# Another order of the same steps on four engines, and no bounds checks on fifteen loaded beginnings

## The chip, the cores and the metric

The kernel runs on one core of a Trainium2 chip. The metric is device time in microseconds (us) of one execution; the value given for a kernel is the median of several runs. A core has five engines with a queue of instructions each, TensorE (PE), VectorE (DVE), ScalarE (ACT), GpSimd (POOL) and SyncE (SP), and they meet only through semaphores.

## The reference, cut to what matters

Tokens `x` (2 x 1024 x 256) pass a cross attention with 16 heads over 77 keys, a feed-forward layer, a second cross attention with one head, and a layer in which each position goes through one of eight matrices, chosen by its position alone.

```python
x = x + _L0_xattn_ref(_layernorm(x), ctx_768, ...)   # 16 heads, 77 keys
x = x + _L0_ffn_ref(_layernorm(x), ...)              # only expert 0 has weight; then a layernorm
x = x + _L1_xattn_ref(_layernorm(x), ctx_768, ...)   # one head; layernorm of x and of the context
x = x + _L1_ffn_ref(_layernorm(x), ...)

# the router of the last layer
scores = jnp.einsum('sp,tp->st', pe, jnp.sign(tile_sigs))
idx = jnp.argmax(scores, axis=-1)
y_all = jnp.einsum('bsd,tod->bsto', x, W) + b
out = jnp.take_along_axis(y_all, idx4, axis=2)[:, :, 0]
```

## The kernel before, in words

The 2048 tokens are cut into eight groups `g` of 256, each with two halves of 128 rows. A group goes through a chain of short steps, and each engine works through **a list of such steps, written out by hand**: TensorE L522 to L552, VectorE L960 to L992, ScalarE L1136 to L1159, GpSimd L1319 to L1332. Each step is a small function that first waits for what it needs, works, and raises a semaphore. SyncE has its own loop of loads. Nothing but these lists and the waits sets the order.

The steps of a group, in the order of the data, with engine and line of VectorE's ones:

- Attention 1. `stats("A", g)` (VectorE, L597), `rs("A", g)` (GpSimd), `apply("A", g)` (one half of the group each on VectorE, L620, and ScalarE) normalise; `tA` (TensorE) transposes; `hi`/`lo("A", g)` (ScalarE/VectorE, L635) split the result in a high and a low part; `q`; `qh`/`ql(g)` (L641) split it; `sc(g, i, a)` scores; `smax` (L651), `ex` (ScalarE), `ssum` (L667), `en(g, i, a)` (GpSimd, L1259, two instructions each) softmax; `tE` transposes; `et`, `pv`, `o`, `wo`; `x1(g)` (L678) adds.
- Feed-forward. `stats`/`rs`/`apply("B", g)`, `tB`, `hi`/`lo("B", g)`; `w1(g, j)` for j = 0 to 3 (L412, twelve matmuls each, as products of high and low parts), `hh` (ScalarE) and `hl(g, j)` (VectorE, L683); `w2(g, i, h)` (L422); `y(g)` (L689), `stats`/`rs("Y", g)`, `x2(g)` (L695).
- Attention 2. `stats`/`rs`/`apply("C", g)`, `tC`, `xtc`, `cs`, `cm`, `cex`, `cp`, `cpt`, `co`, `x3_(g)` (VectorE).
- Last layer. `stats`/`rs`/`apply("D", g)`, `tD`, `xtd`. The tokens are then taken in the order of their matrix, as 15 pairs of (block of 128 tokens, matrix) for each half of the batch: `pc(b, r)` copies a pair's columns, `pr(b, r)` (L457) multiplies, `pa(b, r)` (L741) adds with a mask. Where a pair begins is an integer that the kernel works out itself: `r_pairs` (VectorE, L872 to L910), a chain of some 20 tiny dependent instructions. The last of them write `EV`; `load_starts` (L234) reads fifteen values into registers, on SyncE, and in `starts()` on VectorE (L737) and ScalarE (L1117), with a check of the bounds of each. The weights of the last layer (`load_weights`, SyncE) wait for this.
- Beside the groups: `mask`, `kf`, `kbl(b)` (L772), `vs`, `vb` prepare keys and values of attention 1; the steps that begin with `f_` do so for attention 2; those with `r_` route; `w_hi(n)` (ScalarE, L997) and `w_lo(n)` (GpSimd, L1194) split the weights of the feed-forward layer. The four parts of these weights are loaded in turn into two halves of one buffer, `RAW`: the third load waits for `w_lo(1)`, the fourth (`w2b`) for `w_lo(2)`, and `w_hi(4)` for the fourth.

TensorE writes to four PSUM banks `PB0` to `PB3`, and for `sc` and `tE` to one of two slots `S`. The last argument of a TensorE step is its bank. `hold` keeps the book: before a piece writes to a bank it waits for the step that empties the bank of its last piece (`w1(g, j)` for `hl(g, j)`, `wo(g)` for `x1(g)`, the `w2` of a group for `y(g)`):

```python
for signal, n in let_go.get(at, ()):
    w.wait_ge(s[signal], n)
place[piece] = at
let_go[at] = until
```

## Time and profile before

| | |
|---|---|
| median of 3 runs | 274.83 us (274.80 to 275.03) |
| span of the profiled execution | 271.97 us, 6214 instructions |
| PE busy | 249.2 us, 92% |
| DVE busy | 220.3 us, 81% |
| POOL busy | 189.7 us, 70% |
| ACT busy | 160.7 us, 59% |
| chain that ended last, by engine | PE 68%, DVE 15%, POOL 5%, ACT 5%, issue 4%, DMA 1% |
| mean granted clock of TensorE | 0.982 |

The span is the time from the first to the last instruction in the one execution that the profiler recorded; the runs are timed without the profiler, and some time around the span belongs to them. Busy shares are means over the whole span; the stages differ.

How to read the rows further down: an engine's timeline gives start, duration, engine, line, operation, tiles and shapes of each group of equal instructions, and in brackets the idle time before it and who ended it. The chain gives, in order of time, the pieces of work that the end of the program can be followed back to. In the table of stretches each engine has its busy time and, in brackets, its instructions. L266 are the products with high and low parts (`w1`, `w2`), L259 the plain ones (`q`, `wo`, `f_q`, `cs`), L339 the transposes of groups, L377 `sc`, L387 `tE`, L399 `pv`.

### The profile page before, as it was taken

The page shows a single profiled execution, that of the slowest core. Times are in us where ns is not written, and L with a number is a line of the kernel's source. Part 1 is how long each engine was busy: PE and PEld are TensorE (multiplying, and loading weights), DVE is VectorE, ACT ScalarE, POOL GpSimd, SP SyncE. Part 2 cuts the span into 40 slices and gives each one's busy share as a digit, 9 for nine tenths or more (in the row PEclk, how much of TensorE's full clock was granted, in tenths as well). Part 3 has the DMA queues.
Part 4 walks back from the last instruction along what each step waited for, and adds up shares of the span by engine and source line. Part 5 has one row for each costly group of instructions (what it writes and reads, how often), then busy time and mean ns, then how long its engine had stood idle before and what let it go on. Part 6 is the DMA issues. An engine that isn't in the chain of part 4 may idle for free.

```text
span 272.0 us, 6214 instructions
## 1 busy us (share of the span) xinstructions
PE 249.2 (92%) x2048; PEld 221.2 (81%) x2048; DVE 220.3 (81%) x573; ACT 160.7 (59%) x510; POOL 189.7 (70%) x361
## 2 busy tenths in 40 slices
...
DMA packets 11156, 17.61 MB, mean 65 GB/s; under 512 B 1377, under 2 KB 7509, under 8 KB 11125
## 3 DMA queue, kind: packets, MB, share of 16 engines
...
## 4 chain that ended last, share of the span: by engine, by line
PE 68%; DVE 15%; POOL 5%; ACT 5%; issue 4%; DMA 1%; SPq 0%; POOLq 0%; DVEq 0%; ACTq 0%
PE PB L266 29%; PE PB L259 12%; PE PB L464 9%; PE S L387 5%; PE PB L339 5%; PE PB L399 4%; PE S L377 4%; ACT E L1066 2%; DVE SX L659 2%; POOL E L1263 1%; DMA WKV<-in_w_k 1%; DVE SX L673 1%; POOL SM L1220 1%; DVE HL L686 1%; DVE XTL L638 1%
## 5 line engine op out<-in xcount | busy, mean ns | idle before, releaser
L1263 POOL TENSOR_TENSOR E<-E,SX 128x308 f32<-128x308 f32 x64 | 43.8, 712 | 10.7 <-DVE SX L676 10.4
L1066 ACT ACTIVATE E<-S,SX 128x77 f32<-128x77 f32 x128 | 39.4, 336 | 10.6 <-DVE SX L659 10.6
L266 PE MATMUL PB<-XTH,W1H 128*128 128x256 f32 x128 | 37.7, 295 | 1.5 <-DVE XTL L638 1.4
L266 PE MATMUL PB<-W2H,HH 128*128 128x256 f32 x128 | 37.6, 294 | 0.0
L266 PE MATMUL PB<-XTL,W1H 128*128 128x256 f32 x128 | 36.2, 283 | 0.0
L266 PE MATMUL PB<-XTH,W1L 128*128 128x256 f32 x128 | 36.2, 282 | 0.0
L266 PE MATMUL PB<-W2H,HL 128*128 128x256 f32 x128 | 35.5, 278 | 0.0
L266 PE MATMUL PB<-W2L,HH 128*128 128x256 f32 x128 | 35.5, 278 | 0.0
L1220 POOL TENSOR_TENSOR SM<-SM,nhalf 128x2 f32<-128x2 f32 x40 | 28.3, 707 | 3.1
L1089 ACT ACTIVATE HH<-PB 128x512 fp32r<-128x512 f32 x32 | 19.0, 598 | 18.0 <-PE PB L266 18.0
L1076 ACT ACTIVATE EW<-S 124x640 f32<-124x640 f32 x32 | 21.9, 711 | 10.9 <-PE S L387 10.1
L1066 ACT ACTIVATION_READ_ACCUMULATOR E<-S,SX 128x1 f32 x128 | 27.9, 218 | 0.0
L266 PEld LDWEIGHTS PB<-XTH,W1H 128*128 128x128 f32 x128 | 24.4, 191 | 2.3 <-DVE XTL L638 1.6
L615 DVE BATCH_NORM_STATS2 SM<-X 128x6 f32<-128x256 f32 x64 | 23.8, 413 | 2.1 <-DMA X<-in_x 1.3
L659 DVE TENSOR_REDUCE SX<-S 128x8 f32<-128x616 f32 x32 | 24.4, 783 | 1.0 <-PE S L377 1.0
L266 PEld LDWEIGHTS PB<-W2H,HH 128*128 128x128 f32 x128 | 24.1, 188 | 1.3 <-issue 1.2
L266 PEld LDWEIGHTS PB<-XTL,W1H 128*128 128x128 f32 x128 | 24.5, 191 | 0.1
L266 PEld LDWEIGHTS PB<-XTH,W1L 128*128 128x128 f32 x128 | 24.5, 191 | 0.0
L1033 ACT ACTIVATE XN<-X,SM 128x256 f32<-128x256 f32 (+1 forms) x32 | 18.6, 601 | 9.7 <-POOL SM L1226 9.7
L266 PEld LDWEIGHTS PB<-W2L,HH 128*128 128x128 f32 x128 | 24.1, 189 | 0.1
L1217 POOL TENSOR_TENSOR SM<-SM,eps 128x2 f32<-128x2 f32 x32 | 6.6, 205 | 25.3 <-DVE SM L618 25.1
L266 PEld LDWEIGHTS PB<-W2H,HL 128*128 128x128 f32 x128 | 24.0, 188 | 0.0
...
## 6 DMA issues: line engine op xcount, KB each, us to landing
RAW<-in_w SPq DMA_DIRECT2D x4, 512.0 KB, 6.3
...
X<-in_w1r SPq DMA_DIRECT2D x1, 512.0 KB, 6.6
...
```

The lines of the kernel that those rows point to most:

```text
L259: t = e.matmul(dst, a, b, start=j == 0, stop=j == len(pairs) - 1)
L266: t = e.matmul(dst, a, b, start=first and j == 0, stop=last and j == n - 1)
L339: t = e.transpose(P[:, c * 256 + i * 128:c * 256 + (i + 1) * 128], xn[:, i, c * 128:(c + 1) * 128], ident[:, :])
L464: t = e.matmul(P[:, v * 256:(v + 1) * 256], XP[:, TURN[b, r] % 2, v, c * 128:(c + 1) * 128], weights_of(n)[:, c * 256:(c + 1) * 256], star ...
L615: step(e.bn_stats(smi(K, g, i, 0, 6), src[:, i, :]))
L659: e.tensor_reduce(top, sv, AX, ALU.max, negate=True).then_inc(s["mx"], 1)
L1033: e.activation(dst_of(K, g)[:, 1, 0:n], src_of(K, g)[:, 1, 0:n], ACT.Identity, bias=smi(K, g, 1, 10, 11), scale=smi(K, g, 1, 9, 10)).then_ ...
L1066: t = e.activation(Ei[:, h * NK:(h + 1) * NK], P[:, at:at + NK], ACT.Exp, bias=SX[:, i, 0, k:k + 1], accum_out=SX[:, i, 1, k:k + 1])
L1076: e.activation(ET[:, g % 2, a, :, ts], P[0:CW, 0:640].rearrange("p (c t) -> p c t", c=5), ACT.Copy).then_inc(s["et"], 1)
L1089: e.activation(HH[:, 2 * j:2 * j + 2, :], two(bank("w1", g, j)[:, :]), ACT.Relu).then_inc(s["hh"], 1)
L1220: e.tensor_tensor(sm(K, g, 9), sm(K, g, 8), nhalf[:, :], ALU.pow).then_inc(s["rs" + K], 1)
L1263: t = e.tensor_tensor(Eh, Eh, SX[:, i, 2, 8 * a + h:8 * a + h + 4].unsqueeze(2).to_broadcast([128, 4, NK]), ALU.mult)
```

## The change

Two things. The reading of the fifteen beginnings no longer checks their bounds. And the lists of steps on TensorE, VectorE, ScalarE and GpSimd hold the same steps as before in another order (246, 274, 218 and 142 steps), many pieces of TensorE in another bank. SyncE's list stays. No step is added, dropped or changed.

The diff, cut to the places that the text speaks of (in this order: the reading, TensorE old and new, VectorE old and new, ScalarE old and new, GpSimd old and new):

```diff
         def load_starts(e, row, most, at):
 
             values = nc.values_load_multi_w_load_instructions(EV[0:1, row, 0:NP], engines=[e.engine],
-                                                              min_val=0, max_val=most)[1]
+                                                              min_val=0, max_val=most, skip_runtime_bounds_check_because=
+                                                              "a count of 7 comparisons times a positive constant")[1]
...
-            sc(2, 1, 0, 1); sc(2, 1, 1, 0); pv(1, 1); r_perm(1); w1(0, 0, 3); wo(1, 0); w1(0, 1, 2); w1(0, 2, 1)
-            w1(0, 3, 3); f_m(0); tE(2, 0, 0, 0); tA(3, 2); w2(0, 0, 0, 1); tE(2, 0, 1, 1); tB(1, 0); w2(0, 0, 1)
-            w2(0, 1, 0); q(3, 2); w2(0, 1, 1); w1(1, 0, 3); sc(3, 0, 0, 1); sc(3, 0, 1, 0); w1(1, 1, 0); w1(1, 2, 2)
-            tE(2, 1, 0, 0); f_q(3); w1(1, 3, 1); tE(2, 1, 1, 1); f_c(); sc(3, 1, 0, 0); sc(3, 1, 1, 1); pv(2, 0, 0)
-            pv(2, 1); w2(1, 0, 0, 2); w2(1, 0, 1); tA(4, 3); w2(1, 1, 0); w2(1, 1, 1); wo(2, 1); tE(3, 0, 0, 0)
-            f_o(3); tE(3, 0, 1, 1); q(4, 0); tE(3, 1, 0, 1); tA(5, 3); tE(3, 1, 1, 0); pv(3, 0, 1); pv(3, 1)
-            sc(4, 0, 0, 1); sc(4, 0, 1, 0); tB(2, 2); wo(3, 1); q(5, 0); w1(2, 0, 3); w1(2, 1, 1); w1(2, 2, 2)
...
-            cs(5, 3); w1(7, 0, 2); tD(2, 1); w1(7, 1, 3); w1(7, 2, 0); w1(7, 3, 1); cp(5, 3); w2(7, 0, 0, 2); co(5)
-            tD(3, 0); w2(7, 0, 1); w2(7, 1, 0); w2(7, 1, 1); tC(6, 0); tD(4, 3); pr(0, 1, 1); cs(6, 2); pr(0, 2, 3)
...
+            pv(1, 1); sc(2, 0, 1, 1); sc(2, 1, 0, 0); r_perm(2); tB(0, 1); wo(1, 3); tE(2, 0, 0, 1); f_q(1)
+            w1(0, 0, 3); w1(0, 1, 2); w1(0, 2, 0); sc(2, 1, 1, 1); sc(3, 0, 0, 0); f_c(); w1(0, 3, 2); tB(1, 3)
+            w2(0, 0, 0, 1); tE(2, 0, 1, 1); w2(0, 0, 1); w1(1, 0, 0); tE(2, 1, 0, 0); w2(0, 1, 0); w2(0, 1, 1)
+            w1(1, 1, 3); w1(1, 2, 2); tE(2, 1, 1, 1); sc(3, 0, 1, 0); pv(2, 0, 0); pv(2, 1); sc(3, 1, 0, 0)
+            sc(3, 1, 1, 1); w1(1, 3, 0); f_o(3); wo(2, 2); tA(4, 1); w2(1, 0, 0, 0); tE(3, 0, 0, 0); w2(1, 0, 1)
+            q(4, 1); tE(3, 0, 1, 0); w2(1, 1, 0); w2(1, 1, 1); tE(3, 1, 0, 1); tB(2, 3); tE(3, 1, 1, 0); tA(5, 2)
+            sc(4, 0, 0, 1); sc(4, 0, 1, 0); pv(3, 0, 0); pv(3, 1); tC(0, 1); w1(2, 0, 3); w1(2, 1, 1)
...
+            w2(6, 1, 0); w2(6, 1, 1); co(4); tB(7, 1); tC(5, 2); pr(0, 0, 3); w1(7, 0, 0); tD(2, 1); w1(7, 1, 3)
+            cs(5, 2); w1(7, 2, 0); w1(7, 3, 1); w2(7, 0, 0, 3); cp(5, 2); w2(7, 0, 1); tD(3, 1); co(5); w2(7, 1, 0)
+            w2(7, 1, 1); tC(6, 1); cs(6, 3); pr(0, 1, 0); tD(4, 1); pr(0, 2, 2); cp(6, 3); tC(7, 0); co(6); cs(7, 2)
...
-            ssum(1, 1, 0); stats("B", 0); r_position(); smax(2, 0, 0); ssum(1, 1, 1); apply("B", 0); smax(2, 0, 1)
-            f_kv(0); f_kv(1); vb(1); lo("B", 0); ssum(2, 0, 0); smax(2, 1, 0); smax(2, 1, 1); kbl(1); r_index()
-            ssum(2, 0, 1); apply("A", 3); hl(0, 0); hl(0, 1); x1(1); ssum(2, 1, 0); stats("B", 1); hl(0, 2); f_m()
-            hl(0, 3); apply("B", 1); lo("A", 3); r_pairs(); lo("B", 1); ssum(2, 1, 1); ql(3); y(0); stats("A", 4)
-            smax(3, 0, 0); smax(3, 0, 1); hl(1, 0); apply("A", 4); stats("Y", 0); f_q(); hl(1, 1); x2(0)
-            ssum(3, 0, 0); ssum(3, 0, 1); hl(1, 2); hl(1, 3); f_c(); stats("C", 0); smax(3, 1, 0); smax(3, 1, 1)
-            lo("A", 4); stats("A", 5); stats("A", 6); y(1); apply("A", 5); x1(2); ssum(3, 1, 0); ssum(3, 1, 1)
-            stats("B", 2); f_o(); stats("Y", 1); stats("A", 7); ql(4); apply("B", 2); x2(1); lo("A", 5); smax(4, 0, 0)
...
-            smax(5, 0, 0); ssum(4, 0, 1); lo("B", 3); ssum(4, 1, 0); cm(0); ssum(4, 1, 1); apply("C", 1); starts()
...
-            apply("C", 5); x3_(4); lo("B", 7); apply("D", 2); y(6); stats("D", 4); cm(5); hl(7, 0); stats("Y", 6)
-            hl(7, 1); apply("D", 3); x2(6); hl(7, 2); hl(7, 3); stats("C", 6); x3_(5); stats("D", 5); apply("C", 6)
...
+            smax(1, 1, 1); ssum(1, 1, 0); lo("A", 3); r_expert(); smax(2, 0, 0); f_kv(0); ssum(1, 1, 1); x1(0)
+            f_kv(1); stats("B", 0); ssum(2, 0, 0); r_position(); apply("B", 0); ql(3); smax(2, 0, 1); lo("B", 0)
+            smax(2, 1, 0); x1(1); r_index(); f_m(); ssum(2, 0, 1); stats("B", 1); ssum(2, 1, 0); f_q(); hl(0, 0)
+            hl(0, 1); smax(2, 1, 1); f_c(); apply("B", 1); smax(3, 0, 0); hl(0, 2); hl(0, 3); lo("B", 1)
+            ssum(2, 1, 1); stats("A", 4); r_pairs(); hl(1, 0); ssum(3, 0, 0); hl(1, 1); smax(3, 0, 1); y(0)
+            hl(1, 2); smax(3, 1, 0); ssum(3, 0, 1); stats("Y", 0); apply("A", 4); hl(1, 3); x2(0); f_o()
+            ssum(3, 1, 0); stats("A", 5); lo("A", 4); stats("C", 0); x1(2); smax(3, 1, 1); stats("B", 2)
+            apply("C", 0); ssum(3, 1, 1); apply("B", 2); kbl(1); apply("A", 5); ql(4); y(1); smax(4, 0, 0)
+            stats("A", 6); lo("B", 2); stats("Y", 1); lo("A", 5); smax(4, 0, 1); stats("A", 7); hl(2, 0); hl(2, 1)
...
+            x2(5); hl(6, 0); hl(6, 1); starts(); hl(6, 2); stats("C", 5); hl(6, 3); apply("C", 5); stats("D", 2)
...
+            lo("B", 7); pa(0, 0); apply("D", 3); stats("D", 4); hl(7, 0); cm(5); stats("Y", 6); hl(7, 1); hl(7, 2)
+            hl(7, 3); x2(6); stats("C", 6); x3_(5); stats("D", 5); apply("C", 6); apply("D", 4); y(7); stats("Y", 7)
...
-            ex(1, 1, 1); et(1, 0, 0); et(1, 0, 1); et(1, 1, 0); f_ct(); apply("B", 0); w_hi(4); ex(2, 0, 0)
-            et(1, 1, 1); hi("B", 0); apply("A", 3); o(1); ex(2, 0, 1); ex(2, 1, 0); hh(0, 0); hh(0, 1); ex(2, 1, 1)
...
-            starts(); hi("A", 4); o(2); ex(3, 1, 0); ex(3, 1, 1); apply("C", 0); et(3, 0, 0); apply("A", 5)
...
+            f_ct(); hi("A", 3); et(1, 0, 0); w_hi(2); ex(1, 1, 1); w_hi(3); ex(2, 0, 0); et(1, 0, 1); et(1, 1, 0)
+            qh(3); et(1, 1, 1); o(1); apply("B", 0); w_hi(4); hi("B", 0); ex(2, 0, 1); et(2, 0, 0); ex(2, 1, 0)
...
+            apply("B", 4); cpt(1); ex(5, 1, 1); et(5, 0, 1); hi("A", 7); xtc(2); hi("B", 4); et(5, 1, 0); starts()
...
-            setup(); rs("A", 0); rs("A", 1); bo(0); rs("A", 2); r_iota(); w_lo(1); bo(1); en(0, 0, 0); en(0, 0, 1)
-            en(0, 1, 0); f_rs(); en(0, 1, 1); w_lo(2); f_gb(); en(1, 0, 0); en(1, 0, 1); en(1, 1, 0); rs("A", 3)
-            rs("B", 0); en(1, 1, 1); w_lo(3); w_lo(4); en(2, 0, 0); bo(2); en(2, 0, 1); en(2, 1, 0); rs("B", 1); gx(4)
...
+            setup(); rs("A", 0); rs("A", 1); r_iota(); rs("A", 2); en(0, 0, 0); en(0, 0, 1); bo(0); en(0, 1, 0)
+            rs("A", 3); f_rs(); en(0, 1, 1); w_lo(1); f_gb(); en(1, 0, 0); bo(1); en(1, 0, 1); en(1, 1, 0); w_lo(2)
+            en(1, 1, 1); rs("B", 0); en(2, 0, 0); w_lo(3); w_lo(4); en(2, 0, 1); rs("B", 1); gx(4); en(2, 1, 0)
```

## Rows read from the trace of the kernel before

**Rows 1.** Stretches: us, busy PE, PEld, DVE, ACT, POOL; PE clock, DMA share, GB/s.
```profile
30.20:72.20 42.00, 39.00 (x379) 33.22 (x379) 39.64 (x103) 28.47 (x99) 35.57 (x56) 1.00 0.11 33
100.00:217.60 117.60, 117.60 (x1036) 107.90 (x1025) 94.78 (x238) 73.61 (x242) 86.05 (x167) 1.00 0.18 53
```
**Rows 2.** The chain that ended last, 72 to 104 us: start, us, what.
```profile
72.23 1.69 PE PB L266 x12
73.92 1.09 PE S L377 x12
...
78.61 0.79 PE PB L259 x8
...
87.86 0.44 PE PB L339 x4
88.30 2.73 PE PB L266 x24
...
95.03 0.55 PE S L387 x5
95.58 1.43 PE PB L266 x12
...
98.53 1.93 PE PB L399 x32
```
**Rows 3.** VectorE's timeline, 51 to 76 us.
```profile
51.38 0.69 DVE L638 TENSOR_TENSOR XTL<-PB,XTH 128x512 fp32r<-128x512 f32 x1 [0.58 <-ACT XTH L1041]
...
54.30 1.65 DVE L775 TENSOR_TENSOR KBL<-XTE,mask 128x308 fp32r<-128x308 f32 x2
...
64.12 0.17 DVE L874 SCALAR_TENSOR_TENSOR WD<-WD 128x16 f32<-128x16 f32 x1
...
71.50 0.68 DVE L638 TENSOR_TENSOR XTL<-PB,XTH 128x512 fp32r<-128x512 f32 x1
...
75.31 1.47 DVE L659 TENSOR_REDUCE SX<-S 128x8 f32<-128x616 f32 x2
```
**Rows 4.** VectorE's timeline, 88 to 99 us.
```profile
88.96 0.69 DVE L638 TENSOR_TENSOR XTL<-PB,XTH 128x512 fp32r<-128x512 f32 x1 [1.16 <-ACT XTH L1041]
...
91.44 0.66 DVE L693 TENSOR_TENSOR XN<-PB,XN 128x512 f32<-128x512 f32 x1
...
96.87 0.72 DVE L615 BATCH_NORM_STATS2 SM<-X 128x6 f32<-128x256 f32 x2
...
97.92 0.88 DVE L646 SCALAR_TENSOR_TENSOR XTL<-PB,cols,XTH 128x256 fp32r<-128x256 f32 x2
```
**Rows 5.** VectorE's timeline, 220 to 233 us.
```profile
220.40 0.69 DVE L686 SCALAR_TENSOR_TENSOR HL<-PB,HH 128x512 fp32r<-128x512 f32 x1 [0.50 <-ACT HH L1089]
...
221.72 1.83 DVE L699 SCALAR_TENSOR_TENSOR XN<-XN,SM,bc 128x256 f32<-128x256 f32 x2
...
225.22 1.27 DVE L686 SCALAR_TENSOR_TENSOR HL<-PB,HH 128x512 fp32r<-128x512 f32 x2
...
231.02 0.69 DVE L693 TENSOR_TENSOR XN<-PB,XN 128x512 f32<-128x512 f32 x1 [0.44 <-PE PB L266]
...
232.81 0.91 DVE L699 SCALAR_TENSOR_TENSOR XN<-XN,SM,bc 128x256 f32<-128x256 f32 x2
```
**Rows 6.** TensorE's timeline at 226 us.
```profile
226.04 0.63 PE L339 MATMUL PB<-ident,XN 128*128 128x128 f32 x4 [1.23 <-DVE HL L686]
```
**Rows 7.** Line 236: durations min/median/max in ns, first and last start.
```profile
L236 DVEq FUSED_REGOPS  x15: 183/183/206, 120.9 to 124.8; - x15
```
**Rows 8.** GpSimd's timeline at 32 us.
```profile
32.29 3.18 POOL L1202 TENSOR_TENSOR W1L<-RAW,W1H 128x256 fp32r<-128x256 f32 x4
```
**Rows 9.** The page: costliest groups (busy, mean ns, idle before) and DMA issues.
```profile
L1263 POOL TENSOR_TENSOR E<-E,SX 128x308 f32<-128x308 f32 x64 | 43.8, 712 | 10.7 <-DVE SX L676 10.4
...
RAW<-in_w SPq DMA_DIRECT2D x4, 512.0 KB, 6.3
```
**Rows 10.** ScalarE's timeline at 47 us.
```profile
46.78 1.04 ACT L1006 ACTIVATE W2H<-RAW 128x1024 fp32r<-128x1024 f32 x1
```

152 lines of the change are left out of this document (76 added, 76 removed).

## The prediction

> **What bounds the kernel now.** I began with the busy time of each engine by stage. From 100 to 217.6 us TensorE is busy all of the time; between 30.2 and 72.2 it is VectorE that is nearly full (39.64 of 42.00) while TensorE loses 3 us [rows 1]. In the second stretch only fewer TensorE pieces could help; in the first VectorE's order decides when TensorE gets its operands. Next I followed the chain of waits. It leaves VectorE for the last time before the long stretch at 71.50, with `lo("B", 1)` [rows 3], and from `w1(1, 0)` at 72.23 on it is TensorE's alone until 217.6 [rows 2, 1]. **Where `w1(1, 0)` starts sets all that follows**, as long as nobody makes TensorE wait again. Near the end VectorE is back: TensorE stands 1.23 us before the transpose at 226.04, waiting for a `hl` [rows 6] that is queued behind `x2(6)` [rows 5]. After that a chain of dependent steps of the last group, in the same order in both kernels, sets the end.
>
> **The change part by part.** The sum is made against the profiled execution: its span is 271.97 us, and the median of the runs, 274.83, lies 2.86 above it. I add the 2.86 back at the end.
>
> *Head, VectorE.* All of `r_pairs` stood ahead of `lo("B", 1)`, from 64.12 to 71.50: 7.38 us. It now comes behind. So does `kbl(1)`, 1.57 us from its start at 54.30 to the next step [rows 3]. Ahead of it come `ql(3)` (0.79, as `ql(4)` from 97.92 to 98.71 [rows 4]), one `smax` more (0.74, half of the pair at 75.31 [rows 3]), and the small `f_q` and `f_c` (0.6 together, an estimate from steps of their size): 2.1. VectorE alone would reach the end of `lo("B", 1)` at 72.17 - 8.95 + 2.1 = 65.3, which is 6.9 earlier.
>
> *Head, TensorE.* It does not get there so soon. `lo("B", 0)` ended at 52.07 [rows 3]. Ahead of it there are now `apply("A", 3)` (0.3, half of `y(1)`, which has twice its elements and took 91.44 to 92.01 [rows 4]), `lo("A", 3)` (0.6), `ql(3)` (0.8) and a part of a `ssum` (0.1): 1.8. Then `smax(2, 1, 0)` (0.7) and `x1(1)` (0.6) must be done before `w1(0, 0)` may start, since it is now written to bank 3, which `x1(1)` empties. That gives 55.2, or 54.2 if the idle 0.58 before `lo("B", 0)` [rows 3] and another such wait vanish; I take 55.1. From there to `w1(1, 0)` TensorE has four `w1` of 1.43, two `sc` (1.09 together), `f_c` (0.4, half of the matmuls of `f_q`), `tB(1)` (0.44), two `w2` (2.73) and a `tE` (0.55) [rows 2]: 10.9 us, and 0.3 for starting behind others. So `w1(1, 0)` starts at 66.3 against 72.23: **5.9 earlier**. But more work is left behind it: two `w2` (2.73) went behind, `f_q` (0.79), one `sc` (0.54) and `f_c` came ahead [rows 2], 0.9 to 1.0 more is left. Net **-5.0**. Bounds: VectorE's 6.9 less the same 0.9 is -6.0; if `w1(0, 0)` comes a microsecond later than I say, -4.0.
>
> *Second hold.* TensorE now comes 5 us sooner to `sc(4, 0, 0)`, which needs `ql(4)`. Today `ql(4)` ends at 98.80 [rows 4] and `sc(4, 0, 0)` starts at 100.46, behind the `pv` that began at 98.53 [rows 2]: 1.7 us of slack, less than what TensorE gains. Three `stats` (0.92 to 1.05 each, as 96.87 to 97.92) and `y(1)` (0.57) leave the way to `ql(4)`, 3.5 in all; two `apply` (0.6) enter [rows 4]. So it ends at 95.9 if VectorE gets no faster otherwise, and TensorE would be there at 100.46 - 5.0 - 1.93 (`pv(3)` now behind) + 0.44 (a `tB` now ahead) = 94.0, late by 1.9. Of VectorE's time up to there 1.16, the idle before the step at 88.96 [rows 4], hangs on steps that TensorE feeds and should shrink: 0.7. I take **+1.0**, nearer to 0.7 because that wait is one which TensorE's own lateness makes; ends 0.4 and 1.9.
>
> *End.* `hl(7, 2)` and `hl(7, 3)` now stand ahead of `x2(6)` (221.72 to 225.22 [rows 5]), so the wait of 1.23 us [rows 6] goes. What is late next is `y(7)`. It started at 231.02 with only 0.44 of waiting for TensorE [rows 5], so VectorE was ready at 230.58, and an earlier TensorE can bring it 0.44 and no more, while VectorE's steps from 221.72 on stay the same. And they now start later: `hl(7, 3)` cannot be done before about 1.4 us after the last `w1` of the group, 223.7 on the old clock, where `x2(6)` plus the two `hl` of 0.6 started at 221.72. So `y(7)` comes at 223.7 + (230.58 - 221.72 - 1.2) = 231.4 on the old clock: 0.3 later, unless `x2(6)` loses its slow form. Its first two instructions took 1.83 where those of `x2(7)`, the same shape, took 0.91 [rows 5]; at that price some 1.7 go, TensorE is the last again, and -1.2 is left. I take **-0.3**, nearer to the row as it is; ends +0.3 and -1.2.
>
> The Trainium skill, "SBUF — State Buffer", section "Who interferes with whom", has VectorE and GpSimd share a pair of ports under an exclusive lock, so that the loser stands still. The 1.83 against 0.91 agrees with it, and by this rule `x2(6)` would be as slow wherever GpSimd is at work on it, which would make the end +0.3.
>
> *Bounds checks.* VectorE's sequencer has 15 checks, 183 ns each, between 120.9 and 125.0 [rows 7]; SyncE and ScalarE have as many. All lie where TensorE never stands still [rows 1]: that is the cover, and I take **0**. Without it VectorE's stop, 15 x 0.27 = 4.1 us, would cost what exceeds its lead over TensorE. The reads of the registers on VectorE and ScalarE also move, into the same covered stretch. *Other banks.* A bank has one owner at a time; where a new bank makes a wait that I can place, it is counted (`w1(0, 0)`). For the rest I take 0, between 0 and 0.5.
>
> **Sum**: -5.0 + 1.0 - 0.3 = -4.3; a span of 267.7 and a median of 270.5 us, 1.6% faster.
>
> **Rivals.**
> - *Part is given back.* The second hold costs its 1.9, the end +0.3, and one more step in VectorE's new stretch doubles as `x2(6)` did, 0.8: -5.0 + 1.9 + 0.3 + 0.8 = -2.0, 272.8. For it: VectorE is the full engine up to 72 us [rows 1], so what lengthens there counts. Against: such steps were lengthened before too.
> - *More comes.* TensorE takes VectorE's 6.9 at the head, the second hold is gone, and the end gives its 1.2: -6.0 - 1.2 = -7.2; 267.6. For it: the waits of VectorE that TensorE makes [rows 3, 4]. Against: it needs `w1(0, 0)` at 54.
> - *Slower.* `w_lo(2)` on GpSimd ran from 32.29 to 35.47 [rows 8]. Now `rs("A", 3)` (2), `f_gb` (2) and three `en` of two 0.7 us steps each [rows 9] go ahead of it, besides others ahead of `w_lo(1)`: it ends at about 44. The load into the buffer that it frees lands 6.3 us later [rows 9], `w_hi(4)` waits for that, takes 1.0 [rows 10], and stands on ScalarE ahead of `hi("B", 0)` (0.6), without which there is no `lo("B", 0)`. So `lo("B", 0)` starts 7.9 us after the end of `w_lo(2)` at the earliest: 52, where I count with 53.3. It decides from 45.4 on; at 49.7 the gain of 4.3 is gone, and at 51.7, with GpSimd's steps ahead of it at nearly twice their time, the kernel is 2 slower: 276.8.
> - *No change.* TensorE's waits form anew behind VectorE: what left the way to `lo("B", 1)` is due soon after, and VectorE's work up to `y(2)` is the same. It needs the second hold to be 5 instead of 1. 274.8.
>
> **Chances.** The forecast 0.60, part given back 0.20, more 0.07, slower 0.08, no change 0.05. A measurement of this kernel can tell about 0.2%, 0.55 us, from no change. Faster 0.87, same 0.05, slower 0.08. The range goes from 267.3 (just beyond the second rival: head -6.0, end -1.2, 0.3 of small waits) to 273.5 (head -4.0, hold +1.9, end +0.3, 0.5 for banks: -1.3); outside are the slower case, no change and a tail of the one given back.
>
> **What the profile of the changed kernel would show.** Head: `lo("B", 1)` ends at 65 to 66, `w1(1, 0)` starts near 66.3, `r_pairs` behind them. Hold: TensorE idle for about 1 us before `sc(4, 0, 0)`, at 94 to 96. End: no idle time before the transpose of `tD(3)`; `y(7)` near 226.7 instead of 231.0, held by VectorE's own steps; the last piece on TensorE near 261. No checks on any sequencer. TensorE full from about 97 to 212. It would be wrong if `w1(1, 0)` started after 69, or if TensorE showed new idle time between 100 and 200 us; a `w_hi(4)` that ends after 54 would be the slower case.

## The result, and the profile of the changed kernel

The changed kernel is slower. It took 284.57 us (median of 4 runs, 282.94 to 284.84) beside 274.89 us (4 runs, 274.80 to 275.03) for the kernel before: ratio 1.033 (95% interval 1.031 to 1.036). Run again it took 282.58 us (4 runs, 281.15 to 289.45), ratio 1.028 (1.024 to 1.032). Of the runs of one kernel some are over 1.5% slower than the fastest, at a lower clock (here the one of 289.45 us, in experiment 4 one of 296.65); the ratios leave them out. The forecast was 270.5 us, range 267.3 to 273.5. It had the wrong sign.

The first lines of its page:

```profile
span 283.0 us, 6131 instructions
## 1 busy us (share of the span) xinstructions
PE 253.0 (89%) x2048; PEld 224.2 (79%) x2048; DVE 228.1 (81%) x573; ACT 160.7 (57%) x510; POOL 193.0 (68%) x361
```

The counts of instructions on each engine are those of before; only the register and check instructions are fewer. Yet VectorE is busy 7.8 us longer (228.1 against 220.3) and TensorE 3.8 (253.0 against 249.2). The span has grown by 11.0 us. TensorE works or stands idle, so 3.8 of them are slower work and 7.2 are new idle time. The mean granted clock was 0.970 over 283.0 us against 0.982 over 272.0, which makes some 3.6 us of the 3.8 (an estimate). The table of stretches says where (columns as in [rows 1]; the second fence is the kernel before in the two stretches that its rows don't show):

```profile
5.70:30.20 24.50, 19.26 (x125) 16.84 (x126) 20.49 (x57) 14.25 (x51) 11.60 (x25) 0.93 0.66 195
30.20:72.20 42.00, 36.58 (x329) 30.15 (x328) 36.80 (x84) 27.70 (x93) 31.24 (x49) 0.88 0.10 32
72.20:100.00 27.80, 27.30 (x240) 24.95 (x240) 26.70 (x66) 15.25 (x51) 23.37 (x37) 1.00 0.28 92
100.00:217.60 117.60, 114.74 (x1025) 104.13 (x1024) 98.17 (x242) 74.29 (x244) 89.40 (x172) 1.00 0.15 45
217.60:283.00 65.40, 55.06 (x337) 48.05 (x335) 44.65 (x116) 27.23 (x69) 35.25 (x70) 0.97 0.11 42
```
```profile
5.70:30.20 24.50, 20.48 (x123) 17.13 (x123) 22.54 (x61) 16.82 (x54) 14.35 (x30) 0.86 0.70 217
217.60:272.00 54.40, 44.30 (x262) 38.41 (x260) 36.24 (x92) 23.44 (x62) 29.81 (x53) 0.97 0.10 39
```

TensorE's idle time, stretch less PE: 5.2 us before 30.2 (4.0 in the kernel before), 5.4 from 30.2 to 72.2 (3.0), 0.5 to 100 (0), 2.9 from 100 to 217.6 (0 [rows 1]), 10.3 behind (10.1). So the head costs 3.6 us, the stretch from 72 on, which was full before, 3.4, and the end 0.2.

This is one execution. A second one of the same kernel had its clock at the upper level from 30 to 72 us throughout. Its span was 279.8 us, 7.8 above before: 1.8 more idle time up to 72.2 us, 3.5 from there to 217.6, 0.3 at the end, and 2.2 of slower work. Where a time depends on the clock of the head, this second execution is the better measure, and it is given beside the first.

The head in TensorE's timeline (the kernels without checks have TensorE's lines one higher, L267 for L266 and so on, and the changed kernel VectorE's by one or two):

```profile
39.25 0.47 PE L476 MATMUL PB<-ident,CKN 77*96 77x77 f32 x4 [1.37 <-POOL CKN L1242]
41.40 1.11 PE L340 MATMUL PB<-ident,XN 128*128 128x128 f32 x4 [1.68 <-DVE XN L634]
42.31 3.62 PE L260 MATMUL PB<-Wo,RT 128*128 128x256 f32 x8
...
59.11 0.36 PE L326 MATMUL PB<-WD 128*128 128x16 bf16 x8 [0.71 <-DVE WD L858]
60.76 0.80 PE L340 MATMUL PB<-ident,XN 128*128 128x128 f32 x4 [1.28 <-DVE XTL L648]
```

They are `f_turn`, `tA(3)`, `wo(0)`, `r_perm` and `tB(0)`. `w1(0, 0)` follows at 65.99 (52.75 before, 55.1 forecast), `lo("B", 1)` ends at 75.90 (72.17; forecast 65 to 66) and `w1(1, 0)` starts at 77.33 (72.23; forecast 66.3). In the second execution the three are at 62.50, 72.40 and 73.87. It has these rows for `lo("B", 0)` and `w1(0, 0)`:

```profile
60.26 0.68 DVE L640 TENSOR_TENSOR XTL<-PB,XTH 128x512 fp32r<-128x512 f32 x1
62.50 0.36 PE L267 MATMUL PB<-XTH,W1H 128*128 128x256 f32 x1
```

The third row of the first fence shows TensorE's clock: eight matmuls took 3.62 us, against 1.89 in the second execution. Between 38 and 41.4 us TensorE had worked 0.47 us of 3.4. The clock granted fell to its lower level, 1.2 GHz, for a part of the time: the mean was 0.88 of the full 2.4 GHz in this stretch and 0.70 in the next.

```profile
38.00:41.40 3.40, 0.47 (x4) 0.31 (x5) 3.40 (x5) 2.85 (x17) 3.32 (x6) 0.88 0.51 154
41.40:51.60 10.20, 10.20 (x86) 9.02 (x86) 7.71 (x20) 5.17 (x15) 5.85 (x9) 0.70 0.01 2
```

In the stretch that was full before, TensorE now waits four times, for GpSimd's softmax step once and for VectorE's low parts twice:

```profile
104.27 0.63 PE L340 MATMUL PB<-ident,XN 128*128 128x128 f32 x4 [0.29 <-issue]
105.58 0.76 PE L388 MATMUL S<-ident,E 128*124 128x128 f32 x5 [0.68 <-POOL E L1266]
...
123.64 1.12 PE L260 MATMUL PB<-M,XN 128*128 128x77 f32 x8 [0.74 <-DVE XTL L648]
...
135.12 0.39 PE L267 MATMUL PB<-XTH,W1H 128*128 128x256 f32 x1 [0.93 <-DVE XTL L640]
```

Where 4.1 of VectorE's 7.8 us went, at two places, and below them the answering rows of before. From its start to the next one `apply("A", 3)` took 2.46 us against 0.29, and `r_position` 5.60 against 3.69. `f_norm` took 1.0 more, and the rest is spread over later steps.

```profile
38.81 2.54 DVE L634 TENSOR_SCALAR XN<-X,SM 128x256 f32<-128x256 f32 x1
...
55.79 1.68 DVE L854 TENSOR_TENSOR WD<-WD 128x1024 bf16<-128x1024 f32 x1
57.39 0.75 DVE L855 TENSOR_TENSOR WD<-WD 128x64 f32<-128x64 f32 x1
58.18 0.74 DVE L857 TENSOR_SCALAR WD<-WD 128x64 bf16<-128x64 f32 x1
58.84 0.21 DVE L858 TENSOR_TENSOR WD<-WD 128x64 bf16<-128x64 f32 x1
```
```profile
43.54 1.22 DVE L852 TENSOR_TENSOR WD<-WD 128x1024 bf16<-128x1024 f32 x1
44.69 0.22 DVE L853 TENSOR_TENSOR WD<-WD 128x64 f32<-128x64 f32 x1
44.94 0.26 DVE L855 TENSOR_SCALAR WD<-WD 128x64 bf16<-128x64 f32 x1
...
58.08 0.38 DVE L632 TENSOR_SCALAR XN<-X,SM 128x256 f32<-128x256 f32 x1
```

Beside `apply("A", 3)` GpSimd runs `f_gb`, two instructions of `en(1, 0, 0)` and the first of `bo(1)`. The last four rows of the first fence belong to `r_position`, and beside them GpSimd runs the four pieces of `w_lo(3)`, from 56.35 for 4.13 us. Steps of 64 elements that take 0.22 us alone take 0.75, about as long as one of GpSimd's. The engines do not meet through semaphores alone.

### The profile page after: what moved, and what is told of

It reads as the page before. It is cut to its first block, busy times and chain, and to the rows that moved or that the text cites. A ratio compares the mean times of both kernels' runs of the same rounds, so it can differ in the third digit from the quotient of the medians.

```text
span 283.0 us, 6131 instructions
## 1 busy us (share of the span) xinstructions
PE 253.0 (89%) x2048; PEld 224.2 (79%) x2048; DVE 228.1 (81%) x573; ACT 160.7 (57%) x510; POOL 193.0 (68%) x361
## 3 DMA queue, kind: packets, MB, share of 16 engines
HBM read 14.07 MB, written 3.15 MB: 61 GB/s over the span
## 4 chain that ended last, share of the span: by engine, by line
PE 44%; DVE 29%; issue 8%; DMA 7%; POOL 7%; SPq 1%; ACT 1%; POOLq 0%; DVEq 0%
PE PB L267 16%; PE PB L260 9%; PE PB L465 7%; DVE SM L617 4%; PE PB L340 4%; DMA CKN<-in_ctx 4%; DVE SX L661 3%; PE PB L400 3%; PE S L388 3%; DVE XN L634 2%; PE S L378 2%; POOL E L1266 2%; DVE X L707 2%; POOL SM L1223 2%; DMA X<-in_x,SI 2%
## 5 line engine op out<-in xcount | busy, mean ns | idle before, releaser
L1266 POOL TENSOR_TENSOR E<-E,SX 128x308 f32<-128x308 f32 x64 | 45.6, 735 | 16.1 <-DVE SX L678 15.9
L267 PE MATMUL PB<-XTH,W1H 128*128 128x256 f32 x128 | 38.2, 298 | 0.9 <-DVE XTL L640 0.9
L267 PE MATMUL PB<-W2H,HH 128*128 128x256 f32 x128 | 37.6, 294 | 0.0
L267 PE MATMUL PB<-XTL,W1H 128*128 128x256 f32 x128 | 36.1, 282 | 0.0
L267 PE MATMUL PB<-XTH,W1L 128*128 128x256 f32 x128 | 36.1, 282 | 0.0
L267 PE MATMUL PB<-W2L,HH 128*128 128x256 f32 x128 | 35.6, 278 | 0.0
L267 PE MATMUL PB<-W2H,HL 128*128 128x256 f32 x128 | 35.6, 278 | 0.0
L1078 ACT ACTIVATE EW<-S 124x640 f32<-124x640 f32 x32 | 22.7, 712 | 17.2 <-PE S L388 17.2
L1220 POOL TENSOR_TENSOR SM<-SM,eps 128x2 f32<-128x2 f32 x32 | 7.6, 238 | 29.8 <-DVE SM L620 29.6
L388 PE MATMUL S<-ident,E 128*124 128x128 f32 x160 | 23.4, 278 | 4.3 <-POOL E L1266 2.5
L267 PEld LDWEIGHTS PB<-XTH,W1H 128*128 128x128 f32 x128 | 24.4, 191 | 2.2 <-DVE XTL L640 1.2
L340 PE MATMUL PB<-ident,XN 128*128 128x128 f32 x128 | 20.5, 288 | 5.0 <-DVE XN L634 3.0
L267 PEld LDWEIGHTS PB<-W2H,HH 128*128 128x128 f32 x128 | 24.1, 189 | 0.7 <-issue 0.6
L267 PEld LDWEIGHTS PB<-XTL,W1H 128*128 128x128 f32 x128 | 24.5, 191 | 0.1
L267 PEld LDWEIGHTS PB<-XTH,W1L 128*128 128x128 f32 x128 | 24.4, 191 | 0.0
```

The source lines that it names most:

```text
L267: t = e.matmul(dst, a, b, start=first and j == 0, stop=last and j == n - 1)
L340: t = e.transpose(P[:, c * 256 + i * 128:c * 256 + (i + 1) * 128], xn[:, i, c * 128:(c + 1) * 128], ident[:, :])
L388: t = e.transpose(P[0:CW, c * 128:(c + 1) * 128], E[:, i, a, c * CW:(c + 1) * CW], ident[:, :])
L1078: e.activation(ET[:, g % 2, a, :, ts], P[0:CW, 0:640].rearrange("p (c t) -> p c t", c=5), ACT.Copy).then_inc(s["et"], 1)
L1266: t = e.tensor_tensor(Eh, Eh, SX[:, i, 2, 8 * a + h:8 * a + h + 4].unsqueeze(2).to_broadcast([128, 4, NK]), ALU.mult)
```

## The experiments

Runs of the changed kernel spread by some 2 us within a series, those of before by 1.0 to 2.2. So variants of the changed kernel are compared by places in the trace, and by medians only within one series. The profiled executions differ in the clock of the head, so such a place is compared with both executions of the changed kernel.

**1. The bounds checks alone.** The order of before, with the change to `load_starts`:

```diff
-                                                              min_val=0, max_val=most)[1]
+                                                              min_val=0, max_val=most, skip_runtime_bounds_check_because=
+                                                              "a count of 7 comparisons times a positive constant")[1]
```

> The order of before, only the bounds checks gone. If the checks are covered, as forecast, 274.6 to 275.0 and no sequencer shows them. If they or the earlier load of the last layer's weights matter in themselves, the time moves by more than 0.5 us either way, and the order alone did less or more than the change shows.

275.16 us (10 runs, 274.48 to 275.93), ratio 1.001 (0.999 to 1.003). The checks cost nothing that can be told from zero within 0.3%; all that follows is order.

**2. `r_pairs` alone.** In the order of before:

```diff
-... lo("A", 3); r_pairs(); lo("B", 1) ...
+... lo("A", 3); lo("B", 1) ...
-... f_q(); hl(1, 1); x2(0)
+... f_q(); hl(1, 1); r_pairs(); x2(0)
-... smax(2, 1, 1); kbl(1); r_index()
+... smax(2, 1, 1); r_index()
-... stats("A", 7); ql(4); ...
+... stats("A", 7); kbl(1); ql(4); ...
```

> The order of before, only with r_pairs behind lo("B", 1) and the first two hl of group 1, and kbl(1) just ahead of ql(4). If my step for the head holds (what leaves the way to lo("B", 1) is gained), w1(1, 0) starts at 66 to 68 and the kernel takes 270 to 272. If r_pairs only moves its 7.4 us to the next step that is due (x2, smax, hl of group 1), TensorE waits there instead and the time is 274 to 277.

279.69 us (4 runs), ratio 1.018 (1.015 to 1.021). VectorE and TensorE in this kernel:

```profile
66.18 0.69 DVE L638 TENSOR_TENSOR XTL<-PB,XTH 128x512 fp32r<-128x512 f32 x1 [1.69 <-ACT XTH L1041]
70.64 0.88 DVE L646 SCALAR_TENSOR_TENSOR XTL<-PB,cols,XTH 128x256 fp32r<-128x256 f32 x2 [2.83 <-ACT XTH L1049]
```
```profile
87.70 0.55 PE L266 MATMUL PB<-W2H,HH 128*128 128x256 f32 x1 [4.20 <-DVE HL L686]
```

`lo("B", 1)` came 5.3 us sooner, much as I had reckoned for VectorE alone. `w1(1, 0)` came only 1.3 sooner, at 70.94: TensorE was busy with the pieces ahead of it, without a gap. And behind it TensorE stood 4.2 us: its piece `w2(1, 0, 0)` goes to bank 2, which `hl(1, 2)` empties, and this now waited behind `r_pairs`. The wait did not go; it moved and grew. It also cost the clock. The 24 matmuls behind it ran at the lower level and took 5.2 us, where 24 such took 2.73 in the kernel before [rows 2]:

```profile
87.70:92.90 5.20, 5.20 (x24) 5.20 (x25) 3.77 (x9) 0.00 (x0) 3.65 (x8) 0.50 0.00 0
```

So the price is above both of the ranges expected.

**3. `r_pairs` far behind.** Without checks, at about 140 us, with `starts()` on VectorE and ScalarE and `bs(0)` on GpSimd behind it:

```diff
-... lo("A", 3); r_pairs(); lo("B", 1) ...
+... lo("A", 3); lo("B", 1) ...
-... ssum(4, 1, 1); apply("C", 1); starts()
+... ssum(4, 1, 1); apply("C", 1)
-... ssum(5, 1, 1); apply("C", 2) ...
+... ssum(5, 1, 1); r_pairs(); starts(); apply("C", 2) ...
-... en(4, 0, 0); bs(0); en(4, 0, 1) ...
+... en(4, 0, 0); en(4, 0, 1) ...
```

> The order of before without bounds checks, with r_pairs far behind, at about 140 us, where VectorE has idle time, and with the readings of the registers and the first indirect load of the bias behind it. New theory: TensorE's own work up to w1(1, 0) does not shrink, so the most that can be gained is its idle 1.42 us before w1(1, 0), and the work of 7.4 us is free only here: 272.8 to 273.6. Old theory (VectorE's time off the way to lo("B", 1) is gained): 269 to 271. Rival (the 7.4 us have to be paid on VectorE wherever they stand): 274.5 or more.

282.49 us (4 runs), ratio 1.026 (1.024 to 1.029). Both theories were wrong; the rival (274.5 or more) has the direction, without a price. From 73 to 142 us TensorE ran 0.9 us ahead of the kernel before. Then one wait took 6.6 us:

```profile
148.78 1.09 PE L340 MATMUL PB<-ident,XN 128*128 128x128 f32 x4 [6.58 <-DVE XN L694]
```
```profile
147.62 0.41 DVE L633 TENSOR_SCALAR XN<-X,SM 128x256 f32<-128x256 f32 x1 [1.69 <-issue]
```

It is `tC(2)`, which needs `apply("C", 2)` and a bank that `y(3)` empties; both stood behind `r_pairs` and `starts()`. The edit is no clean case of `r_pairs`: `starts()` now reads its registers right behind it, and 1.69 us of VectorE's lump of 7.74 are that reading (the second row), with 6.0 for `r_pairs`. Behind the wait the granted clock was 0.50 for 5 us more, an estimate of 2.6 us. VectorE has idle time in this stretch (it is busy 94.78 of 117.60 us [rows 1]), but in waits of at most 3.6 us, mostly for TensorE (the trace of experiment 1). Its lead is never 7 us.

**4. The same in the changed kernel** (ScalarE's `starts()` behind `o(5)`, GpSimd's `bs(0)` to `bs(5)` in a row behind `rs("Y", 3)`).

```diff
-... stats("A", 4); r_pairs(); hl(1, 0) ...
+... stats("A", 4); hl(1, 0) ...
-... ssum(5, 1, 1); smax(6, 0, 0) ...
+... ssum(5, 1, 1); r_pairs(); smax(6, 0, 0) ...
```

> The changed kernel, with r_pairs at about 155 us in place of 78 to 86, and what waits for it behind. If TensorE's idle 2.9 us between 100 and 136 come from VectorE being full from 50 to 145 us, of which these 7.6 us are a part, they go, and the kernel takes 281 to 282. If they come from the order around them, 284 to 285.

288.77 us (4 runs), ratio 1.049 (1.045 to 1.053), above both of the ranges expected. From 100 to 139 us TensorE gained 1.3 us on the changed kernel's own course: the wait of 0.93 at 135 went, those at 104, 106 and 124 stayed at 0.23, 0.68 and 0.63. So up to half of that stretch's loss goes with `r_pairs`; then `w1(4, 0)` waited 4.12 us.

**5. TensorE's idle time at 38 to 41 us.** In the changed kernel, one `wo` ahead of the waiting pieces, then both:

```diff
-... f_turn(1); tA(3, 0); wo(0, 2); ...
+... wo(0, 2); f_turn(1); tA(3, 0); ...
-... r_perm(2); tB(0, 1); wo(1, 3); ...
+... wo(1, 3); r_perm(2); tB(0, 1); ...
```

> The changed kernel, only with wo(0) of TensorE ahead of f_turn and tA(3), which it stands idle for between 38 and 41.4 us before the granted clock falls to 1.2 GHz for some 5 us. If that idle time and the clock are what makes the head late, the clock stays at 2.4 GHz in 41 to 52 us, w1(0, 0) comes 3 to 4 us sooner and the kernel takes 280 to 282. If GpSimd and VectorE hold the head up, w1(0, 0) moves by under 1 us and the time stays at 284 to 285.

> The changed kernel with wo(0) ahead of f_turn and tA(3), and wo(1) ahead of r_perm and tB(0), on TensorE. Both wo have their data when TensorE stands idle. If the head is late because TensorE's list has waiting pieces ahead of ready ones, the idle 1.8 us at r_perm and tB(0) go as well: 280.5 to 281.5. If VectorE, which does its routing steps ahead of apply("B", 0), sets the pace, it is as with wo(0) alone, 282.5 to 283.5.

282.90 us (1.031, 1.027 to 1.034) and 282.62 us (1.027, 1.024 to 1.030). The clock stayed at its upper level in 41.4 to 51.6 us with the first edit, and `sc(2, 0, 0)` came 4.7 us sooner than in the first execution of the changed kernel. But `w1(0, 0)` gained only 2.2, half of it there at 29 us already, and 3.6 with both edits. Even this is the clock: the unedited kernel, run again, had no drop of the clock in this stretch, and there `w1(0, 0)` starts at 62.50 and `lo("B", 0)` ends at 60.94, against 62.42 and 60.97 with both edits. Both times `lo("B", 0)` ends behind VectorE's own steps, which had no gap from `r_position` to `apply("B", 0)`. So the order of these pieces ahead of `tB(0)` is not what sets the head. The unedited kernel, run again, had a span of 279.8 us instead of 283.0, but stood idle for 6.1 us here, against 5.4:

```profile
30.20:72.20 42.00, 35.93 (x360) 30.40 (x361) 40.36 (x91) 30.44 (x103) 34.27 (x54) 1.00 0.13 39
```

The clock explains some 3 us of the first profile. It does not explain the sign.

**6. `bo(1)` out of the way of `apply("A", 3)`**, in the changed kernel (on GpSimd ahead of `w_lo(1)`, 8 us sooner).

```diff
-... en(0, 1, 1); w_lo(1); f_gb(); en(1, 0, 0); bo(1) ...
+... en(0, 1, 1); bo(1); w_lo(1); f_gb(); en(1, 0, 0) ...
```

> The changed kernel with bo(1) of GpSimd, two additions, ahead of w_lo(1), about 8 us sooner, so that it no longer stands beside VectorE's apply("A", 3), which took 2.46 us where it took 0.29 in the kernel before. If GpSimd's bo(1) holds VectorE up, the step takes under 1.2 us, tA(3) comes over 1 us sooner and the time falls by 1 to 3 us, the more the clock stays up. If another GpSimd step takes bo(1)'s place beside it, the step stays above 2 us and the time at 283 to 285.

283.64 us (282.03 to 284.67), ratio 1.032 (1.028 to 1.037). VectorE in this kernel, and below it the row of the changed kernel that answers to the first:

```profile
33.60 2.64 DVE L589 SCALAR_TENSOR_TENSOR RAW<-X,nkeep,RAW 128x1024 f32<-128x1024 f32 x1
...
40.10 1.18 DVE L634 TENSOR_SCALAR XN<-X,SM 128x256 f32<-128x256 f32 x1
41.20 0.66 DVE L812 TENSOR_SCALAR WD<-WD 128x8 f32<-128x8 f32 x1
```
```profile
33.67 1.28 DVE L589 SCALAR_TENSOR_TENSOR RAW<-X,nkeep,RAW 128x1024 f32<-128x1024 f32 x1
```

`apply("A", 3)` fell from 2.46 to 1.10 us (each from its start to the next one's, since the durations of rows overlap), as the first theory said, and `pivot(2)`, which now starts beside `bo(1)`, grew by 1.36: the next step starts at 41.20 where it started at 41.27, and the time fell by no more than the spread. In this pair the delay went with GpSimd's instructions, not with the VectorE step. It can also fall on GpSimd: in the changed kernel its `w_lo(1)`, beside `pivot(2)` at 1.28 us and `f_norm`, took 4.05 us, and `w_lo(2)` of the same size 3.15. The Trainium skill ("SBUF — State Buffer", section "Who interferes with whom") describes this as an exclusive lock on a pair of ports that VectorE and GpSimd share; this pair of rows agrees.

**7. GpSimd's additions cut, in both kernels.** `bo`, `b2` and `bd` add two columns instead of 256, so the output lacks these biases; the same edit for each:

```diff
-                    t = e.tensor_tensor(Y[:, i, :], Y[:, i, :], bc[:, B2, :], ALU.add)
+                    t = e.tensor_tensor(Y[:, i, 0:2], Y[:, i, 0:2], bc[:, B2, 0:2], ALU.add)
```

> The order of before, with GpSimd's additions of biases (bo, b2 and bd: 48 instructions of 128 x 256 elements) cut to two columns each, so that 35 us of GpSimd's work are gone; the output lacks these biases. It is the control of the next run: 270 to 274, since the chain of before leaves little of GpSimd's on the way.

> The changed kernel with the same cut of bo, b2 and bd. If VectorE's lengthened steps beside GpSimd (7 us more busy time for the same 573 instructions) are a main part of the loss, it falls to within 6 us of the control and VectorE's busy time comes within 4 us of the control's. If the order of TensorE and VectorE itself is the loss, it stays 8 to 10 us above the control.

271.68 us (0.989, 0.986 to 0.992) and 277.01 us (1.009, 1.006 to 1.012): the gap between the two orders is 5.3 us instead of 8 to 10. The kernel before gained 3.2 us, the changed one 5.6 to 7.6, by the series that it is compared with.

```profile
PE 248.8 (92%) x2048; PEld 221.5 (82%) x2048; DVE 216.1 (80%) x573; ACT 160.9 (60%) x510; POOL 163.9 (61%) x361
```
```profile
PE 250.4 (91%) x2048; PEld 221.8 (81%) x2048; DVE 223.1 (81%) x573; ACT 160.4 (58%) x510; POOL 166.4 (61%) x361
```

The time came out as the first theory said, VectorE's busy time did not: it stays 7.0 us above the control. The two kinds of effect were not told apart, since the cut also frees GpSimd itself. TensorE's wait before `tA(3)` fell from 1.68 to 0.39 us, with an `apply("A", 3)` of 1.26 us. The wait of 0.68 for GpSimd's `en` at 106 us is gone too, and that has nothing to do with VectorE. So GpSimd's additions make up a part of the loss, and more than half is left without them. `r_position` is as long as ever here: the `w_lo(3)` beside it was not cut.

**8. `w_lo(3)` away from `r_position`.** In the changed kernel `w_hi(2)` and `w_hi(3)` ahead of `et(1, 0, 0)` on ScalarE, `w_lo(3)` ahead of `rs("B", 0)` on GpSimd:

```diff
-... hi("A", 3); et(1, 0, 0); w_hi(2); ex(1, 1, 1); w_hi(3) ...
+... hi("A", 3); w_hi(2); w_hi(3); et(1, 0, 0); ex(1, 1, 1) ...
-... rs("B", 0); en(2, 0, 0); w_lo(3); w_lo(4) ...
+... w_lo(3); rs("B", 0); en(2, 0, 0); w_lo(4) ...
```

> The changed kernel, with w_hi(2) and w_hi(3) of ScalarE ahead of et(1, 0, 0), for which it waits 3.9 us, and w_lo(3) of GpSimd right behind en(1, 1, 1), so that VectorE's r_position no longer runs beside it. If r_position's 5.6 us in place of 3.7, and apply("B", 0) behind it, are what the head loses, lo("B", 0) comes 2 us sooner and the kernel takes 282 to 283. If another step is lengthened in their place, the sum stays and it is 283.5 to 285.

281.58 us (280.63 to 283.61), ratio 1.024 (1.020 to 1.028), just under the 282 to 283 of the first case. The changed kernel without the edit took 282.58 in another series.

```profile
54.95 1.22 DVE L854 TENSOR_TENSOR WD<-WD 128x1024 bf16<-128x1024 f32 x1
56.09 0.22 DVE L855 TENSOR_TENSOR WD<-WD 128x64 f32<-128x64 f32 x1
56.35 0.26 DVE L857 TENSOR_SCALAR WD<-WD 128x64 bf16<-128x64 f32 x1
```

These are the steps that took 1.68, 0.75 and 0.74 above. `r_position` fell from 5.60 to 4.31 us, `apply("B", 0)` from 0.77 to 0.33, and `lo("B", 0)` ended at 60.11 instead of 62.91, though only 0.8 before the 60.94 of the second execution, whose clock was better. Counted from the start of `r_position` it is 7.7 us instead of 9.5 and 9.4: a gain of 1.7 to 1.9. Here no other step took the delay over.

**9. Group 3 brought forward, alone.** In the order of before, `stats`, `rs`, `apply`, `tA`, `hi`, `lo`, `q`, `qh` and `ql` of group 3 and `vb(1)` at about the places of the changed kernel, with the banks that this asks for; `r_pairs` where it was. Its core:

```diff
-... smax(1, 1, 0); ql(2); smax(1, 1, 1) ...
+... vb(1); smax(1, 1, 0); ql(2); apply("A", 3); smax(1, 1, 1) ...
-... f_kv(1); vb(1); lo("B", 0) ...
+... f_kv(1); ql(3); lo("B", 0) ...
-... f_turn(0); r_rank(2) ...
+... f_turn(0); tA(3, 1); r_rank(2) ...
-... tE(1, 1, 1, 0); tB(0, 0)
+... tE(1, 1, 1, 0); q(3, 1); tB(0, 0)
```

> The order of before, with the attention steps of group 3 brought forward on all engines to about where the changed kernel has them (stats, rs, apply, tA, hi, lo, q, qh, ql of group 3, and vb(1)), ahead of the feed-forward of group 0; r_pairs stays where it was. If bringing them forward costs the head its time (3.9 us more on VectorE ahead of lo("B", 0), TensorE waiting there), w1(0, 0) comes 3 us or more later, TensorE loses 2 to 4 us more between 30 and 72 us, and the kernel takes 276.5 to 279. If only the places beside GpSimd's long additions cost, and not the order, 274.5 to 275.5.

278.26 us (277.50 to 278.46), ratio 1.012 (1.008 to 1.016).

```profile
30.20:72.20 42.00, 37.44 (x368) 31.63 (x369) 37.27 (x93) 29.54 (x100) 30.36 (x50) 1.00 0.07 22
```
```profile
40.59 2.02 DVE L632 TENSOR_SCALAR XN<-X,SM 128x256 f32<-128x256 f32 x1
```

`w1(0, 0)` started at 59.14 (2.0 us of that were there at 29 us already) against 52.75, TensorE lost 4.6 us in this stretch against 3.0, and 5.7 before it against 4.0. The latter says little, since the order of before had 5.5 there in experiment 1. This one edit costs 3.2 us, without `r_pairs` being touched, as the first case expected. The second row shows the same lengthening of `apply("A", 3)`, at a place where it meets GpSimd.

**10. The two small steps of the end.** `hl(7, 2)` and `hl(7, 3)` ahead of `x2(6)`, and the last `pr` in bank 0 or out of it (the first two in the kernel before, the third in the changed kernel):

```diff
-... x2(6); hl(7, 2); hl(7, 3) ...
+... hl(7, 2); hl(7, 3); x2(6) ...
```

```diff
-... pr(1, 7, 3)
+... pr(1, 7, 0)
```

```diff
-... pr(1, 7, 0)
+... pr(1, 7, 2)
```

> The order of before, only with hl(7, 2) and hl(7, 3) ahead of x2(6) on VectorE. By my step for the end, the wait of 1.23 us before tD(3) goes and y(7) comes 0.3 later to 0.44 sooner: 274.3 to 275.2, no change that can be told. If the wait before tD(3) is worth its length: 273.5 to 273.8.

> The order of before, only with the last piece pr(1, 7) in bank 0, as in the changed kernel. If the bank alone makes the wait (pa(0, 7) must empty it first): 275.9 to 276.2, 1.1 to 1.2 us above before. If the wait comes from the order around it: within 0.3 of before.

> The changed kernel, only with the last piece pr(1, 7) in bank 2 in place of bank 0, which pr(0, 7) holds until VectorE's pa(0, 7). If the bank makes the wait of 1.25 us before it, the end comes 1.2 us sooner: 283.2 to 283.5. If the last pa is held by VectorE itself, within 0.3 of the changed kernel.

`b_hl_ahead` took 274.70 us (12 runs), ratio 1.000 (0.998 to 1.002). The wait before `tD(3)` was gone, and 1.72 us stood before `tC(6)` in its place (0.38 before):

```profile
225.96 0.60 PE L339 MATMUL PB<-ident,XN 128*128 128x128 f32 x4
232.52 0.85 PE L339 MATMUL PB<-ident,XN 128*128 128x128 f32 x6 [1.72 <-ACT XTE L1113]
```

`b_bank0` took 275.25 us (12 runs), ratio 1.002 (1.000 to 1.003), although the trace has the expected wait:

```profile
266.60 1.10 PE L464 MATMUL PB<-OWN,XP 128*128 128x256 f32 x4 [1.24 <-DVE X L752]
```

Expected was 1.1 to 1.2 us. GpSimd's queue was still issuing the stores ahead of the last one, each 0.96 us and 0.30 apart, and the last one waited 0.35 instead of 0.30, which covers the wait. `a_bank2` took 282.15 us (279.71 to 283.83). In its trace the last store stands at 275.45, 3.28 us sooner than in the first execution of the changed kernel, but at 275.50 in the second, whose bank is the old one. So the bank gave nothing there either; the difference is the clock in the head.

**11. Repairs.** The edits of 5 (both) and 8 together, beside the changed kernel on the same chip; and a better use of what 2 and 3 showed: in the order of before without checks, `r_pairs` cut in two, the first 3.7 us where they were, the last (expected at 3.1 us, 4.1 in the trace) ahead of `y(2)`, `starts()` behind (on ScalarE behind `o(5)`, and GpSimd's `bs(0)` behind `rs("Y", 3)`).

```diff
+            def r_pairs_2():
+
                 step(e.tensor_scalar(B[:, 2, :], B[:, 2, :], PI[:, 0:1], None, ALU.is_le))
...
-... apply("C", 1); starts()
-            y(2); hl(3, 0); stats("Y", 2); smax(5, 0, 1) ...
+... apply("C", 1); r_pairs_2()
+            y(2); hl(3, 0); stats("Y", 2); starts(); smax(5, 0, 1) ...
```

> The changed kernel with both wo moved ahead on TensorE (as in a_wo_both) and the split of the weights moved forward (as in a_wlo3_early). If the two repairs add up: 279 to 280.5. If both only shift the same wait: 281 to 282. It stays above before in either case, since the steps of group 3 are still ahead of the feed-forward of group 0.

> The changed kernel once more, on the same chip and beside the same runs of before as the two others: 282.9 to 284.9.

> The order of before without bounds checks, with r_pairs cut in two: 3.7 us of it stay ahead of lo("B", 1), where TensorE is not yet there, and 3.1 us go to just ahead of y(2), where VectorE waited 3.6 us for TensorE in b_rpairs_late; the readings and the first load of the bias behind. If small portions in VectorE's waits are free and the idle 1.42 us before w1(1, 0) is all there is to gain, TensorE runs 0.9 to 1.4 us ahead from 72 us to the end: 273.5 to 274.2. If it is paid back, 274.8 or more.

280.57 us (278.94 to 281.34), ratio 1.020 (1.017 to 1.023) to before, against 282.58 (1.028) for the changed kernel: 1 to 2 us come back. That is between the two cases expected, and in its trace `w1(1, 0)` stands at 73.69 against 73.87. The changed kernel itself came out below the range that I had expected for it. `b_rpairs_split` took **273.77 us** (8 runs, 273.12 to 274.11) beside 274.78, ratio 0.996 (0.995 to 0.998): the only kernel here that beats both.

```profile
30.20:72.20 42.00, 40.29 (x393) 34.33 (x392) 38.41 (x100) 28.57 (x99) 34.68 (x55) 1.00 0.12 33
```

TensorE loses 1.7 us in this stretch instead of 3.0, no wait stands before `w1(1, 0)`, and from 100 to 217.6 us it loses 0.3.

## Why the prediction was wrong

**The step that failed** is "Head, TensorE": `w1(0, 0)` at 55.1 us, where it started at 62.50 and 65.99 in the two executions. From there to `w1(1, 0)` the prediction was right (11.2 us; 11.4 and 11.3). Two terms of the step were wrong.

- *TensorE's own list.* Ahead of `w1(0, 0)` it now has `tA(3)`, `q(3)`, `f_m`, `wo(1)`, a `tE` and `f_q`, which took 6.1 us in the second execution and 8.1 at the clock of the first. The prediction took them out from behind `w1(0, 0)` and put them nowhere. They were in the diff. A test that needs no experiment would have shown the error: both orders hold the same TensorE work, so at `w1(1, 0)` nothing can be gained but idle time, and the idle time just ahead of it was 1.42 us, and 3.0 in the whole stretch [rows 1]. A gain of 5.0 was more than there was. Experiment 2 has 1.3 gained there, `b_rpairs_split` what can be kept of it (1.0 at the end).
- *VectorE's steps ahead of `lo("B", 0)`*, put at 1.8 us more. From the start of `lo("A", 2)` (31.48 us, and 31.20 in the second execution) to the start of `lo("B", 0)` they took 9.2 more: 3.9 for the steps of group 3, since `apply("A", 3)` took 2.46 where I had 0.3; 3.4 by which `r_position` (+1.9), `f_norm` (+1.0) and `apply("B", 0)` (+0.5) are longer, for which I had counted nothing; 3.7 for `pivot(2)` and the routing steps `r_ranks` and `r_expert`, which used to stand ahead of `lo("A", 2)` and which I had overlooked; less 0.9 for `stats("A", 3)` and 1.0 of idle time that went (9.1 in all). So a gain at the head was not only too large but not there: `w1(1, 0)` came 1.6 us late in the second execution and 5.1 in the first, with 1.0 of work more left behind it.

All three of my own signs were there in both executions: `w1(1, 0)` after 69, new idle time between 100 and 200 us, and a `w_hi(4)` that ends after 54.

**"VectorE alone would reach `lo("B", 1)` 6.9 earlier"** had the removal right (5.3 in experiment 2 with `ql(3)` not ahead) and forgot the bill. VectorE is nearly full to 100 us, and what leaves one step is due at the next one. I had named this in the rival of no change, at 0.05, with "what left the way is due soon after". Experiment 2 shows it to be worse than no change: a wait of 4.2 us and the lower clock behind it.

**The port between VectorE and GpSimd** was in the prediction as 0.8 us in a rival and as a reason why `x2(6)` stays slow; it should have been a term for every VectorE step in a full stretch.

**The second hold** was foreseen as one wait of 1.0 before `sc(4, 0, 0)`. There was none there. There were four behind, 0.29 to 0.93, 2.6 us together, with VectorE nearly full (60.7 of 64 us from 72 to 136). It was foreseen for a TensorE that comes 5 us sooner; TensorE came later, and the waits came all the same. So that new waits came in this stretch is right, and the reason given for them is not.

**The end**: the wait before `tD(3)` went and `y(7)` was held by VectorE, as forecast; worth -0.3 by the sum and 0 within 0.2% by experiment 10. **The bounds checks**: 0 within 0.3%, by experiment 1.

**The slower rival** named the right sign by a last step that did not decide. `w_lo(2)` did come late, ending at 51.9 us and not at 44, since it waited 2.6 us for `w_hi(2)`, which stood on ScalarE behind `et(1, 0, 0)`; and `w_hi(4)` ended at 59.5. But `hi("B", 0)` then waited 2.1 us more, for `tB(0)` and VectorE's `apply("B", 0)`. The late split of the weights cost by what it lengthened on VectorE (experiment 8), not by its own chain. That chain is next in line: in experiment 8 `hi("B", 0)` followed `w_hi(4)` at once.

**The sum as it was**, against 11.0 us in the profiled execution: 3.6 new idle time before 72 us, 3.4 between 72 and 217.6, 0.2 at the end, 3.8 of slower TensorE work, mostly by the clock. By causes, as far as single edits show them: group 3 ahead 3.2; GpSimd's additions 2 to 4 more than in the old order, in part on VectorE and in part through GpSimd's own queue; `w_lo(3)` beside `r_position` 1.7 to 1.9 on the place of `lo("B", 0)`. They overlap and don't add up exactly, and no edit here gives the whole 8 to 10 us: the head is explained by the sum above, and the cause of the new waits between 72 and 217.6 us stays open in part.
